# A four-stage attention and feed-forward kernel: the second feed-forward layer goes batch by batch, with norm, keys and queries of the next attention in its second half

## What is computed

```python
def _conn_dense(kernel_bool, x):                       # weights are +1 or -1
    return x @ jnp.where(kernel_bool, 1.0, -1.0)
h = jnp.concatenate([x, -x], axis=-1)
h = jax.nn.relu(s0 * _conn_dense(k0, h)) * 2           # 256 -> 1024
h = jax.nn.relu(s1 * _conn_dense(k1, h)) * 2           # 1024 -> 1024, "the second layer"
h = s2 * _conn_dense(k2, h)                            # 1024 -> 256
...
x = x + jnp.tanh(g_ffn[0]) * _L0_ffn_ref(_layernorm(x, axis=-1), ...)
x = x + jnp.tanh(g_xattn[1]) * _L1_xattn_ref(_layernorm(x, axis=-1), ctx_768, ...)   # 16 heads of 64, 1024 keys
```

## Time and profile before

| | |
|---|---|
| three runs, median (lowest to highest) | 1206.12 us (1204.16 to 1210.72) |
| the profiled execution: its time, its span | 1207.47 us, 1205.6 us |
| PE busy | 1083.3 us, 90% of the span |
| DVE, ACT, POOL busy | 867.0, 696.9, 275.4 us |
| mean granted PE clock | 0.967 |

### The profile page before, as it was taken

One profiled execution on the slowest core, in us unless ns is written; L12 is line 12 of the kernel. 1 busy time (PEld: TensorE's weight loads), 2 busy tenths in 40 slices (PEclk: granted clock), 3 DMA queues, 4 the chain that ended last, 5 costly groups with the idle time before them and its releaser, 6 DMA issues. The chain is left out here.

```text
span 1205.6 us, 20215 instructions
## 1 busy us (share of the span) xinstructions
PE 1083.3 (90%) x6824; PEld 948.7 (79%) x6824; DVE 867.0 (72%) x1485; ACT 696.9 (58%) x1269; POOL 275.4 (23%) x292
## 2 busy tenths in 40 slices
PE   1869988898799789999989999899999879999998
PEld 1758877687588668898978888788978767888887
DVE  6689956898422588888969888788888664555555
ACT  2467756675622468777767777687777422323222
POOL 5050004100146310402040201202020212343441
PEclk9889989899899989999999999999999989999999
DMA  5000000001111000000100010000000004443432
GB/s 156 1 5 1 1 2 1 1 2 64 46 51 34 8 1 2 1 2 2 36 3 1 1 36 1 3 2 1 28 1 1 27 5 121 112 115 98 122 103 72
DMA packets 18046, 38.18 MB, mean 32 GB/s; under 512 B 3777, under 2 KB 10049, under 8 KB 17441
## 3 DMA queue, kind: packets, MB, share of 16 engines
q1 hardware_dynamic: 17952, 37.01, 10.5%
HBM read 35.76 MB, written 1.25 MB: 31 GB/s over the span
## 5 line engine op out<-in xcount | busy, mean ns | idle before, releaser
L274 PE MATMUL PS<-R 128*128 128x512 f32 (+2 forms) x2728 | 631.9, 377 | 50.7 <-issue 15.6
L274 PEld LDWEIGHTS PS<-R 128*128 128x128 f32 x2728 | 461.2, 196 | 129.7 <-issue 23.8
L1316 DVE TENSOR_TENSOR R<-PS,R 128x512 fp32r<-128x512 f32 x352 | 224.4, 682 | 38.4 <-ACT R L1046 37.4
L1046 ACT ACTIVATE R<-PS 128x512 fp32r<-128x512 f32 x352 | 191.1, 596 | 82.0 <-PE PS L618 81.5
L1020 ACT ACTIVATE FA<-PS,nmax 128x1024 f32<-128x1024 f32 (+1 forms) x160 | 192.4, 1202 | 37.5 <-DVE nmax L1305 26.8
L629 PE MATMUL PS<-R 128*128 128x256 f32 x1408 | 203.2, 290 | 8.9 <-DVE FB L1324 8.6
L618 PE MATMUL PS<-eye,FA 128*128 128x128 f32 x1408 | 189.3, 279 | 11.5 <-ACT FA L1020 5.0
L618 PEld LDWEIGHTS PS<-eye,FA 128*128 128x128 f32 x1408 | 164.5, 143 | 44.2 <-DVE R L1316 11.2
L629 PEld LDWEIGHTS PS<-R 128*128 128x128 f32 x1408 | 179.1, 190 | 16.4 <-issue 12.9
L1305 DVE TENSOR_REDUCE nmax<-PS 128x1 f32<-128x1024 f32 x128 | 155.7, 1220 | 44.3 <-PE PS L274 26.2
L429 POOL TENSOR_SCALAR R<-R 64x512 fp32r<-64x512 f32 x40 | 26.0, 650 | 348.2 <-ACT R L1167 287.8
(11 more groups left out here) (163 smaller groups left out, 981.4 us busy)
## 6 DMA issues: line engine op xcount, KB each, us to landing
FB<-comb SPq DMA_DIRECT2D x48, 256.0 KB, 3.8
wst<-we_in SPq DMA_DIRECT2D x26, 384.0 KB, 4.0
wst<-w_in SPq DMA_DIRECT2D x4, 1024.0 KB, 4.8
wst<-w_in SPq DMA_DIRECT2D x3, 512.0 KB, 6.5
x<-x_in SPq DMA_DIRECT2D x2, 512.0 KB, 5.8
FB<-ctxT_in SPq DMA_DIRECT2D x2, 512.0 KB, 4.5
FB<-k_in SPq DMA_DIRECT2D x8, 128.0 KB, 2.0
FB<-ctxT_in SPq DMA_DIRECT2D x4, 256.0 KB, 4.0
```

The lines of the kernel that those rows point to most:

```text
L274: last = mm(out, a, b, start=(n == 0), stop=(n == len(passes) - 1), skip_group_check=skip)
L1046: a_(L.pt[0][:, (u // 2) % 2, 4 * g_:4 * g_ + 4, (u % 2) * P:(u % 2) * P + P], L.turn(u, g_).rearrange("p (t n) -> p t n", t=4), ACT.Copy) ...
L1316: inc(v.tensor_tensor(lo, turned, hi.bitcast(F32), ALU.subtract), "p_lo")
```

## The change

The second layer goes batch by batch: jobs 0 to 7 are the eight tiles of batch 0, jobs 8 to 15 the same tiles of batch 1. So `h1` is laid out by batch, each tile of weights is loaded and converted twice (16 refills of `fw1`/`fw2` instead of 8, still in two buffers, now `j % 2`), and F2 uses two banks instead of four. The first F2 waits for the first layer of batch 0 alone. The banks and results of batch 0 are complete after F3(7), so DVE adds them to x (`ffn_out(0)`) and takes the norm of batch 0 in jobs 8 to 13, and PE gets jobs of the next attention: one key job behind each of F3(8) to F3(11), the transposes of the norm behind F3(12), the queries behind F3(14) and F3(15). What stays behind the layer is the values and `first_scores`. The norm of batch 1 moves into the first units of `block(2, 0)`: statistics at unit 2, root on ACT at unit 3, scaling at unit 4, and the transposes and splits at units 5 to 8. POOL's other work is spread over the refills.

```diff
+CONTEXT_AT = {1: 0, 3: 2, 11: 1, 14: 3}
@@ POOL
-        for m in range(MT):
-            pool.wait_ge(s[f"k1_in{m % 2}"], 32 * (m // 2 + 1))
-            if m >= 2:
-                pool.wait_ge(s["f3_done"], AHEAD_F3 + 2 * m - 2)
...
+        for j in range(2 * MT):
+            r, n = j % 2, 512 * (j - 5)
+            pool.wait_ge(s[f"k1_in{r}"], 32 * (j // 2 + 1))
+            if j >= 2:
+                pool.wait_ge(s["f3_done"], AHEAD_F3 + j - 1)
+            step(g.tensor_scalar(fw1[:, r].rearrange("p k n -> p (k n)"), k12b[:, r, 0:FF], 2.0, -1.0, ALU.mult, ALU.add))
+            step.wait()
+            g.tensor_scalar(fw2[:, r], k12b[:, r, FF:FF + D], 2.0, -1.0, ALU.mult, ALU.add).then_inc(s["fw1_ready"], 1)
+            if j in CONTEXT_AT:
...
+            elif j == 13:
+                pool.wait_ge(s["fw1_ready"], j + 1)
+                pair1_low(2, 3)
@@ PE
+        def ffn2(j):
+            h, r = j // MT, j % 2
+            if j % MT == 0:
+                pe.wait_ge(s["f_lo"], MT * (h + 1))
+            pe.wait_ge(s["fw1_ready"], j + 1)
+            pe.wait_ge(s["f_act"], 2 * MT + j - (3 if j < 2 else 1))
...
+        ffn2(0)
+        for j in range(2 * MT):
+            if j + 1 < 2 * MT:
+                ffn2(j + 1)
+            ffn3(j)
...
+            if 8 <= j < 12:
+                first_project(range(j - 8, j - 7))
+            elif j == 12:
+                pe.wait_ge(s["pj_lo"], 4)
+                ln_turn(3 * NB + 1, HIDDEN_TURN)
+            elif j == 14:
+                pe.wait_ge(s["ln_lo"], 4 * NB + 2)
+                first_project(range(4, 5))
+            elif j == 15:
+                first_project(range(5, 6))
@@ ACT, in block(2, 0)
+                if not late:
+                    if u == 3:
+                        ln_root(3 * NB + 2)
@@ DVE, in block(2, 0)
+                if not late:
+                    if u == 2:
+                        dve.wait_ge(s["x_ffn"], 2)
+                        norm_statistics(x_tiles(1))
+                    elif u == 4:
+                        dve.wait_ge(s["xc_lo"], 4)
+                        norm_apply(3 * NB + 2, x_tiles(1), mid_rows)
@@ DVE, ahead of block(2, 0)
+        first_lo(range(4, 5))
         ffn_out(1)
...
+        first_lo(range(5, 8))
         maximum(L1, NB, 0)
...
+        first_lo(range(8, 14))
         block(2, 0, late=False)
```

More of the change, by code:

```diff
@@ L346, in _ @@
             ffn_load(c)
[L347 to L352, removed]
+        for j in range(2, 2 * MT):
+            sp.wait_ge(s["fw1_ready"], j - 1)
+            ffn_load(j)
+            if j in (4, 14):
+                sp.wait_ge(s["xc_lo"], 1 if j == 4 else 3)
+                context_load(2 if j == 4 else 3)
         sp.wait_ge(s["w1o_split"], 1)
@@ L802, in _ @@
             group(PS[:, j % 4, :], passes).then_inc(s["f1_done"], 1)
[L804 to L835, removed]
         def project(b, J0, jobs, order=NEXT_ORDER, banks=NEXT_BANKS, freed=NEXT_FREED):
@@ L877, in fill @@
                     out_project(L1, 1 - b, C - 1, (w,), (5, 5))
+                if not late and u in (5, 7):
+                    kt = u // 2 - 2
+                    pe.wait_ge(s["ln_xn"], 3 * NB + 2)
+                    if kt == 1:
+                        pe.wait_ge(s["ln_lo"], 4 * NB + 3)
+                    for t in range(TT):
+                        last = nc.tensor.transpose(PS[:, 5, t * P:t * P + P], mid_rows[t][:, kt * P:kt * P + P], eye_ap)
+                    last.then_inc(s["ln_turned" if kt else "ln_half"], 1)
                 if more and u == UNITS - 2:
+                    if not late:
+                        pe.wait_ge(s["ln_lo"], 4 * NB + 4)
+                        pe.wait_ge(s["xc_lo"], 4)
                     if wq is not None:
@@ L1148, in _ @@
             h, m = j // MT, j % MT
-            a_(h1[0][:, m, h * 512:h * 512 + 512], PS[:, j % 4, :], ACT.Relu, scale=tg[:, 4:5]).then_inc(s["f_hi"], 1)
+            a_(h1[h][0][:, m, :], PS[:, j % 4, :], ACT.Relu, scale=tg[:, 4:5]).then_inc(s["f_hi"], 1)
             a_(hf[:, j % 2, :], PS[:, j % 4, :], ACT.Relu, scale=tg[:, 4:5]).then_inc(s["f_act"], 1)
[L1151 to L1154, removed]
-                a_(fh2[:, c % 2, 0, :], PS[:, c, :], ACT.Relu, scale=tg[:, 5:6]).then_inc(s["f_hi"], 1)
-                act.wait_ge(s["f_lo"], 2 * MT + 4 * i + c - 1)
-                a_(hf[:, c % 2, :], PS[:, c, :], ACT.Relu, scale=tg[:, 5:6]).then_inc(s["f_act"], 1)
         def project_hi(C, J0, jobs, order=NEXT_ORDER, banks=NEXT_BANKS):
@@ L1176, in project_hi, with first_hi, block @@
                 ins.then_inc(s["pj_hi"], 1)
-        def block(C, b, more=True):
+        def first_hi(jobs):
+            project_hi(NB, 0, jobs, FIRST_ORDER, FIRST_BANKS)
+        for j in range(2 * MT):
+            act.wait_ge(s["f2_done"], j + 1)
+            act.wait_ge(s["f3_done"], AHEAD_F3 + j - 1)
+            a_(fh2[:, j % 2, 0, :], PS[:, j % 2, :], ACT.Relu, scale=tg[:, 5:6]).then_inc(s["f_hi"], 1)
+            act.wait_ge(s["f_lo"], 2 * MT + j - 1)
+            a_(hf[:, j % 2, :], PS[:, j % 2, :], ACT.Relu, scale=tg[:, 5:6]).then_inc(s["f_act"], 1)
+            if 9 <= j < 13:
+                first_hi(range(j - 9, j - 8))
+            if j == 10:
+                ln_root(3 * NB + 1)
+            elif j == 13:
+                ln_split(2 * NB + 1, 0, LNH, HIDDEN_TURN)
+        def block(C, b, late=True, more=True):
             J1 = 14 * (C - 1)
             def fill(u):
+                if not late:
+                    if u == 3:
+                        ln_root(3 * NB + 2)
+                    elif u in (6, 8):
+                        kt = u // 2 - 3
+                        act.wait_ge(s["ln_turned" if kt else "ln_half"], 2 * NB + 2 if kt else 1)
+                        a_(LNH[:, kt, S:2 * S], PS[:, 5, :], ACT.Copy).then_inc(s["ln_hi"], 1)
                 if more:
```

180 lines of the change are left out of this document (100 added, 80 removed).

## The result

The changed kernel takes 1224.03 us in the median of its runs (1220.73 to 1228.51). The kernel before, timed beside it, takes 1206.41 (1204.16 to 1210.72). The ratio is 1.0148 with an interval of 1.0120 to 1.0176: the change costs 17.6 us. The profiled execution of after took 1228.51, with a span of 1226.7 against 1205.6 before, so 21.1 more; it is the slowest run of after, 4.5 above its median.

What follows compares the result with a forecast made beforehand. PE bounds the second layer and never waits there, with slack behind it. Terms -4.6 + 34.0 + 3.2 - 17.3 + 5.5 = +20.8 on a median of 1206.1 gave 1227 us, range 1213 to 1242.

Steps and rivals of the forecast that it cites:

- start of the layer: Second layer's start: F2(0) needs only the first half's rests, so F2(0) and F2(1) end at 329.60, gaining 4.6 us.
- 14 refills: F2(2) to F2(15): each waits for a whole refill released by F3(j-2), 2.18 plus 0.25 restart; 34.0 us lost.
- PE's clock in the gaps: Nine open waits ahead of F2: two clock falls of 1.6 us each, 3.2 lost; bounds none to 14.4.
- gap behind the layer: F3(14) to the block's third transposes: 41.1 us shrinks to 22.2, less 1.6 for low clock; 17.3 gained, between 14 and 18.9.
- norm in the block: First attention block: batch 1's norm now stands where PE and DVE are full; 5.5 us lost, between 3.5 and 7.
- the 0.25 taken: PE's restart after each refill wait: between 0.06 and 0.36 us, taken as 0.25 because two waits stand there.
- the long form: Refill beside a DVE instruction: locked out, 2.18 us in every refill, sum 34.0; without it 14 x 0.32 = 4.5 would go.
- the 2.4 named as a sign: Profile after: F2 rows with about 2.4 us idle before them, released by POOL's L501, 14 times.
- two falls, since 2.43 is nearer to 2.22: Nine open gaps: idle 2.43 lies between 2.98 (clock fell) and 2.22 (clock kept); two falls of 1.6 us, 3.2 lost.
- a sign of being wrong: Profile after, second layer: forecast wrong if PE's largest releaser isn't POOL or the clock row stands well under 0.95.
- The bound of 3.5: Batch 1's norm in the first attention block: lower bound of the loss, without the low clock within the earlier 6.17 us.
- refills covered: Pair F3(j-2), F2(j): if F2(j) needs no such late refill, the 34.0 and 3.2 go, -16.4, 1190 us; chance 0.05.

Runs made afterwards that it cites:

- the kernel with its keys apart: Against the kernel with three weight buffers: `pair1_low` spread over refills 12 and 13, batch 0's bias added behind the layer; 1191.08 us.
- without the root: Against the changed kernel: a copy replaces the square root of batch 1's norm, so ACT's two table loads go; 1223.34 us (two runs).
- the kernel before with a late refill: Against the kernel before: refills 2 to 7 released by F3(2m-2), directly ahead of their F2, not by F3(2m-3); 1226.52 us, ratio 1.0157.
- filled gaps: Against the changed kernel: five idle products, result never read, in each of the nine open waits of the layer; 1217.72 us, ratio 1.0107.
- the split release: Against the changed kernel: still two buffers, `fw1` released by F2(j-2) and only `fw2` by F3(j-2); 1202.89 us, ratio 0.9968.
- the three kernels with three buffers: The changed kernel with a third weight buffer alone (1190.58 us), with `pair1_low` also divided (1191.08), or with F2(0) waiting for all 16 rests (1194.43).

## Why the prediction was right, and which terms were mis-sized

The forecast was 1227 us for a measured 1224.03, within its range, and slower as forecast. The deciding step, the refill between F3(j-2) and F2(j), is shown by three runs: taken away in the new order (three buffers, -33), for the greater part taken away with two buffers (-21), and put alone into the old order (+21).

Against the profiled execution, by the terms of the sum:

| term | predicted | profile | what differed |
|---|---|---|---|
| start of the layer | -4.6 | -3.5 | zeroing products at 322.35, not 321.19 |
| 14 refills | +34.0 | +33.1 | 2.32 each, and 0.6 once behind `pair1_low` |
| PE's clock in the gaps | +3.2 | +6.4 | four falls, not two |
| gap behind the layer | -17.3 | -17.8 | |
| norm in the block | +5.5 | +3.9 | no low clock in it |
| sum | +20.8 | +22.1 | |

The layer lost another 0.3 beyond these terms, and the span grew by 21.1 in all, so 1.3 came back behind the block, in code that the change doesn't touch. Part of it is in the last block: the products that took 1.69 at the lower clock before take 1.19 in the timeline of after, behind the same idle, and that block's last transposes are 20.0 us later than before and not 22.4; 1.1 is lost again behind them. That the sum, +20.8, comes within 0.3 of the 21.1 is luck: the clock cost 3.2 more than predicted, the start gained 1.1 less and 0.3 of the layer had no term, and refills, gap, norm and the part behind the block gave 4.3 back.

```profile
943.01 1.19 PE L642 MATMUL PS<-R 128*128 128x256 f32 x8 [1.94 <-DVE FB L1364]
```

*Start.* The gain was as worked out (32 products in 7.42 with their tail), but the layer itself began 1.16 us later. In the runs with the new order, these products began anywhere from 318.42 to 322.35, and with three buffers alone at 321.16 where the kernel with its keys apart, the same up to there, has 318.42, so that term has a spread of its own, and the earlier trace rows is one draw of it.

*Refills.* The length was read from the earlier trace rows and came out as read: 1.05 and 0.72, the latter beside a DVE instruction of 1.26. From PE's release (331.46) to POOL's end (333.63) are 2.17 against the 2.18 read. The restart was shorter than the 0.25 taken: 0.05 to the first product, and 0.10 in a slightly longer F2 (3.76 instead of 3.66). By the Trainium skill, "SBUF — State Buffer", section "Who interferes with whom", the long form should repeat in each refill. Of the fourteen in after, thirteen took 0.72 and one, behind `pair1_low`, 0.41, so the trace agrees. The idle that the profile shows ahead of F2 is 2.06 and not the 2.4 named as a sign, since it is counted from the tail of F3; nine rows have 2.06 to 2.13, and the others less because a key job or the transposes stand inside.

*Clock.* This is the term that was mis-sized, and it was the step "two falls, since 2.43 is nearer to 2.22". The idle was 2.06, shorter than the gap that had kept the clock (before, the 5 us behind the stretch of the earlier trace rows were at 1.00 as well), and yet four of nine fell here, three of nine in the same layer without the root, and five of six in the kernel before with a late refill. One row of a gap that kept its clock was not enough to price nine. Each fall cost 1.6, as taken. The clock row of the layer is 0.94, at the edge of what I had called a sign of being wrong. The falls may also be what differs between runs: the profiled one, with a mean clock of 0.965, lies 4.5 us above the median, and the others have 0.968 to 0.972, but these are means over the whole kernel, and only the profiled run shows where its clock fell. The median's difference, 17.6, is smaller than the predicted 20.8, though the profile's, 21.1, is not.

*Gap.* The first transposes of the block came 17.8 us behind F3(14) (452.63), where 16.7 and up to 1.6 for a low clock had been added up, and the third 23.3 where that gives 23.8. The low clock is there: 0.72 from 448 to 454 us.

*Norm.* The rows of the last block hold a stretch at the lower clock (6.17 us to the next transposes); here that was 3.91. The bound of 3.5 that I had worked out without the low clock was the better value, and the run without table loads shows that ACT's loads are 0.6 of it; the rest is put down to DVE by the timeline alone.

*The rival "refills covered".* It was priced at 1190 and a kernel that covers them measured 1190.58, but the price was too simple: key jobs and the transposes of the norm, four times 1.15 and 1.04, lie in the waits and are free only as long as these are there. Without the waits they cost 5.6, which gives 1195 by my own terms, so that 1190 was met is luck. Up to the end of the block the trace agrees with the 1195: start -4.7, layer +7.8, gap -18.6, block +4.0, together -11.4, where these terms give -10.8. The span, though, is 17.1 below that of before. The other 5.7 came behind the block, in code that none of the edits touches; some of it is again products that stand at the lower clock in the trace of before (the same 1.69 of the earlier trace rows is 1.19). From the next block's first transposes to the end are 709.6 us before, 708.3 in after, 706.4 with filled gaps, 705.4 without the root, 708.0 with the split release, and 703.6 to 704.6 in the three kernels with three buffers. So the 1.3 of after is within what equal code varies by; why the kernels with three buffers lie below all others stays open.

## What to carry to other kernels

When a loop is reordered so that each buffer is refilled twice as often, ask for every buffer which instruction reads it last and what stands between that and the next one to use it; if nothing does, the whole refill lies on the path, however idle the engine that makes it. Two remedies worked here: release each part of the buffer by its own last reader (1202.89 us), or take a third buffer from space that is dead by then (1190.58, 1.1% below the kernel before). A wait of PE that comes back every few microseconds can be paid twice, once as the wait (2.2 us here) and once as products at the lower clock behind it (1.6 here, four times of nine). And an engine that is mostly idle can still be late, when work that must wait for others stands ahead of the refill in its order (POOL idle for 7.00 us ahead of a late refill).

## What was unexpected of the hardware

The same wait of 2.06 us ahead of the same 16 products was followed by the full clock in one job and by the lower one in the next, with 1.6 us between them: four of nine times in after, three of nine and mostly in other jobs in a second run of the same layer (the one without the root), and five of six in the kernel before with a late refill, where waits of 2.06 to 2.14 us stand 13 us apart. With five products in each gap, and 0.90 to 0.97 us idle behind them, it never happened in nine. So it does not hang on the job alone; which of two equal gaps is followed by a fall stays open.
